# Perceiver block on one core: second-half attention scores placed directly ahead of the first value products, values computed in pairs, start-up loads cut smaller

## The reference

```python
x = x + xattn(layernorm(x), ctx)     # 32 query heads, 8 KV heads, head width 128, RoPE
x = x + attn(layernorm(x))           # 32 heads of width 16, biases
x = x + ffn(layernorm(x))            # base product + gated low-rank experts (8 of rank 16)
# xattn, for each KV head and its 4 query heads:
q, k, v = rope(xn @ Wq.T), rope(ctx @ Wk.T), ctx @ Wv.T
a = softmax(where(causal, q @ k.T * 128**-0.5, min))
out += (a @ v) @ Wd.T
```

## Time and profile before

| what | value |
|---|---|
| median of three runs | 716.91 us (lowest 716.67) |
| the profiled execution's own time | 717.73 us |
| its span, first to last instruction | 715.7 us |
| TensorE busy | 705.5 us, 99% |
| VectorE, GpSimd, ScalarE busy | 512.8, 472.1, 372.8 us |
| mean busy share of the 16 DMA engines on the loads' queue | 21.5% |

### The profile page before, as it was taken

How to read it: one execution, slowest core, us unless ns; L and a number is a source line. 1 busy time by engine, 2 the same in 40 slices (tenths; PEclk the granted TensorE clock), 3 DMA queues, 4 the chain that set the end, 5 groups by cost and what they waited for, 6 DMA issues and landing times.

```text
span 715.7 us, 12890 instructions
## 1 busy us (share of the span) xinstructions
PE 705.5 (99%) x4848; PEld 563.6 (79%) x4848; DVE 512.8 (72%) x814; ACT 372.8 (52%) x559; POOL 472.1 (66%) x360
## 2 busy tenths in 40 slices
PE   8999999899999999999999999999999999999998
PEld 6788878677778788787778778777788888887886
DVE  5665897957857857757767767758667888889735
ACT  5555665644644643743743743743336677765220
POOL 1898145777776877867867867844624889985730
PEclk9999999999999999999999999999999999999999
DMA  7554513411310310311301301300300110011003
GB/s 273 207 166 144 170 51 103 162 49 41 118 45 16 117 44 19 113 43 42 103 31 44 103 29 60 104 1 16 103 0 2 45 31 31 2 41 50 16 1 117
DMA packets 25560, 51.08 MB, mean 71 GB/s; under 512 B 2352, under 2 KB 10672, under 8 KB 25520
## 3 DMA queue, kind: packets, MB, share of 16 engines
q1 hardware_dynamic: 25520, 50.53, 21.5%
HBM read 40.04 MB, written 10.49 MB: 71 GB/s over the span
## 4 chain that ended last, share of the span: by engine, by line
PE 86%; DVE 6%; ACT 2%; DMA 2%; issue 2%; POOL 1%; SPq 0%; DVEq 0%; ACTq 0%
PE pj L1583 11%; PE sc L1674 11%; PE pj L1674 10%; PE pj L1773 9%; PE tp L1583 8%; PE pv L1661 5%; PE sc L1641 4%; PE tp L1674 4%; PE pj L1951 3%; PE pv L1569 3%; PE sc L1823 2%; PE tp L1836 2%; PE pv L1847 2%; PE tp L1557 2%; PE pj L1557 2%; PE tp L1648 2%
## 5 line engine op out<-in xcount | busy, mean ns | idle before, releaser
L494 POOL TENSOR_TENSOR sw<-sw,cst 128x512 f32<-128x512 f32 x72 | 102.4, 1422 | 39.5 <-ACT sw L671 39.4
L518 POOL TENSOR_TENSOR sm<-sm,mx 128x512 f32<-128x512 f32 x64 | 72.0, 1131 | 40.7 <-DVE mx L1209 27.3
L523 POOL TENSOR_TENSOR sm<-sm,rz 128x512 f32<-128x512 f32 x64 | 66.7, 1057 | 24.1 <-DVE rz L1224 24.1
L500 POOL TENSOR_TENSOR qr<-t,sw 128x512 f32<-128x512 f32 x54 | 73.5, 1362 | 7.7
L1583 PE MATMUL tp<-x,w 128*128 128x512 f32 x288 | 76.3, 401 | 1.2 <-ACT sw L671 0.8
L793 ACT ACTIVATE sm<-sm 128x512 f32<-128x512 f32 x64 | 40.3, 633 | 61.9 <-POOL sm L518 61.9
L512 POOL TENSOR_TENSOR w<-raw,w 128x896 fp32r<-128x896 f32 x24 | 50.4, 2120 | 33.1 <-ACT w L656 33.1
L1773 PE MATMUL pj<-xh,ws 128*128 128x512 f32 x192 | 64.6, 402 | 0.2 <-ACT kb L891 0.2
L1583 PEld LDWEIGHTS tp<-x,w 128*128 128x128 f32 x288 | 51.9, 188 | 11.8 <-ACT sw L671 1.0
L656 ACT ACTIVATE w<-raw 128x1792 fp32r<-128x1792 f32 x15 | 25.6, 1707 | 59.8 <-DVE raw L1099 59.8
L1228 DVE TENSOR_TENSOR cl<-pv,ch 128x1024 fp32r<-128x1024 f32 x32 | 39.1, 1222 | 23.2 <-ACT ch L801 23.2
(11 more groups left out here) (274 smaller groups left out, 1850.4 us busy)
## 6 DMA issues: line engine op xcount, KB each, us to landing
rawd<-in_w_d SPq DMA_DIRECT2D x16, 512.0 KB, 3.2
raw<-in_w_q SPq DMA_DIRECT2D x15, 512.0 KB, 3.3
kscr<-sm SPq DMA_DIRECT2D x16, 256.0 KB, 2.1
vscr<-sm SPq DMA_DIRECT2D x16, 256.0 KB, 2.6
kr<-kscr SPq DMA_DIRECT2D x8, 512.0 KB, 3.3
vv<-vscr SPq DMA_DIRECT2D x16, 256.0 KB, 2.6
raw<-in_w_k SPq DMA_DIRECT2D x4, 512.0 KB, 6.2
cT<-in_ctxT SPq DMA_DIRECT2D x4, 512.0 KB, 7.2
```

The costliest lines, as they stand in the source:

```text
L494: pool.tensor_tensor(bs(sw[par][:, :]), bs(sw[par][:, :]), rep(cst[:, C_SIN:C_SIN + S], HB), ALU.mult).then_inc(sin_done, 1)
L500: pool.tensor_tensor(o, bs(t1[par][:, :]), bs(sw[par][:, :]), ALU.add).then_inc(rope, 1)
L518: pool.tensor_tensor(s3, s3, per_group(mx[:, c, :], 8), ALU.subtract).then_inc(subbed, 1)
L523: pool.tensor_tensor(s3, s3, per_group(rz[:, c, :], 8), ALU.mult).then_inc(normed, 1)
```

## The change

- **Order in a head on TensorE.** Scores 2 and 3 move from behind the second product to behind S3, directly ahead of values 0. Values 0 and 1 follow each other, and so do values 2 and 3. Transposes 1 move ahead of S3, transposes 3 ahead of S3'.
- **Banks.** Values 1 are written into `tp` (B_BANK and T_BANK), values 3 into `sc`, and `c_hi` and `c_lo` read there. C_BANK and B_BANK trade places, and `out_x` gets other banks; waits are moved to match.
- **The other engines' orders** in `head` follow: the masks of chunks 2 and 3 stand behind c_mix and t1_q of k = 1, their exp between the high parts of values 0 and 1, their subtract_max between GpSimd's RoPE steps.
- **Start.** The first weight piece is loaded in halves and the first half of ctx in four slices of 256 KB; the constants are loaded earlier; the first K tiles multiply the parts in another order; seven fewer warm-up matmuls.
- **First head's queries and head 0.** first_swap(1) ahead of block_hi(6), the two c_add ahead of both first_t1, w7_sum(3) ahead of the last first_add, and another order of VectorE's work at the beginning of head 0.

```diff
@@ -34,7 +34,7 @@
 SCH = 4
 NSU = 2 * KT
 UNITS = [(0, 0), (1, 0), (0, 1), (1, 1), (2, 0), (3, 0), (2, 1), (3, 1)]
-WARM_UP = 16
+WARM_UP = 9
 C_ID, C_COS, C_SIN, C_MASK, C_PAR = 0, 128, 192, 256, 320
 NCONST = 322
 
@@ -119,7 +119,7 @@
...
@@ -268,9 +269,9 @@
 
 
         k_bank = [pj[:, 0, :], pj[:, 1, :], tp[:, 0, :], tp[:, 1, :]]
-        A_BANK, B_BANK, C_BANK, T_BANK = pj[:, 0, :], pj[:, 1, :], tp[:, 1, :], tp[:, 0, :]
-        O_BANK = [B_BANK, sc[:, 0, :], sc[:, 1, :], B_BANK, sc[:, 0, :], sc[:, 1, :], B_BANK, C_BANK]
-        O6_BANK = [B_BANK, sc[:, 0, :], sc[:, 1, :], B_BANK, sc[:, 0, :], A_BANK, B_BANK, C_BANK]
+        A_BANK, B_BANK, C_BANK, T_BANK = pj[:, 0, :], tp[:, 1, :], pj[:, 1, :], tp[:, 0, :]
+        O_BANK = [pv[:, 0, :], pv[:, 1, :], B_BANK, sc[:, 0, :], B_BANK, pv[:, 0, :], pv[:, 1, :], C_BANK]
+        O6_BANK = [pv[:, 0, :], pv[:, 1, :], B_BANK, sc[:, 0, :], B_BANK, A_BANK, B_BANK, C_BANK]
         O7_BANK = [B_BANK, A_BANK, C_BANK, B_BANK, A_BANK, C_BANK, B_BANK, C_BANK]
 
 
...
@@ -374,13 +375,14 @@
             def load_d(g, i):
                 sp.dma_start(rawd[i][:, :], w_d[g, i]).then_inc(s_rd[i], 16)
 
-            load_piece(0)
-            load_ctx(0, 0)
-            load_ctx(0, 1)
+            sp.dma_start(raw2[0][:, 0:512], w_k[0][:, 0:512]).then_inc(s_wa, 16)
+            for k in range(KT):
+                load_ctx(k, k, 1, 0)
+            sp.dma_start(raw2[0][:, 512:1024], w_k[0][:, 512:1024]).then_inc(s_w[0], 16)
             load_piece(1)
-            load_ctx(1, 0)
-            load_ctx(1, 1)
             sp.dma_start(cst[:, :], consts).then_inc(s_const, 16)
+            for i in range(2):
+                load_ctx(KT + i, 2 * i, 2, 1)
             sp.wait_ge(plo_d, 1)
             load_piece(2)
             sp.wait_ge(plo_p, 1)
...
@@ -557,13 +559,15 @@
                     subtract_max(4 * g + c, c)
                 for c in range(2):
                     normalise(4 * g + c, c)
-                for c in range(2, 4):
-                    subtract_max(4 * g + c, c)
                 for p in range(2):
                     for k in range(4):
                         rope_sin(k % 2, ri(2 * n + p, k))
+                        if p == 0 and k == 1:
+                            pool.wait_ge(scored, 4 * g + 4)
                         if more or p == 0 or k < 2:
                             rope_add(k % 2, ri(2 * n + p, k), q_out(p, k))
+                        if p == 0 and k < 2:
+                            subtract_max(4 * g + 2 + k, 2 + k)
                     if p == 0:
                         for c in range(2, 4):
                             normalise(4 * g + c, c)
...
@@ -708,12 +720,16 @@
                 act.wait_ge(stp, n)
                 act.activation(dst[:, :], bank, ACT.Copy).then_inc(pcp, 1)
 
-            piece_hi(0)
+            first_hi(0, s_wa, phi_a)
             ctx_hi(0, range(KT))
+            first_hi(1, s_w[0], phi)
             piece_hi(1)
             ctx_hi(1, range(KT))
+            swap_k(0)
             piece_hi(2)
-            for t, i in PHASE1:
+            swap_k(1)
+            piece_hi(3)
+            for t, i in PHASE1[2:]:
                 if t == "k":
                     if i == 4:
                         act.wait_ge(kproj, 6)
...
@@ -769,8 +783,8 @@
             block_hi(5)
             part_copy(pcb, 3, B_BANK)
             first_swap(0, C_BANK)
+            first_swap(1, T_BANK)
             block_hi(6)
-            first_swap(1, T_BANK)
             part_copy(u2, 5, A_BANK)
             part_copy(u2b, 6, B_BANK)
             part_copy(pc, 7, C_BANK)
...
@@ -819,27 +833,25 @@
                 if first:
                     turn(0, 0)
                     wdhi(g, 0, wdh)
-                    part_copy(u2, 14 * n + 3, A_BANK)
-                    p_copy(q, 0)
-                    part_copy(pc, 14 * n + 4, C_BANK)
-                    exp(q + 2, 2, X_SCALE)
-                    wdhi(g, 1, wdh)
                 else:
                     act.wait_ge(stp, 14 * n + 2)
                     wdhi(g, 0, wdh)
                     turn(0, 0)
-                    wdhi(g, 1, wdh)
+                    p_copy(q, 0)
                     part_copy(u2, 14 * n + 3, A_BANK)
-                    exp(q + 2, 2, X_SCALE)
+                if first:
+                    part_copy(u2, 14 * n + 3, A_BANK)
                     p_copy(q, 0)
-                    part_copy(pc, 14 * n + 4, C_BANK)
+                part_copy(pc, 14 * n + 4, C_BANK)
+                p_copy(q + 1, 1)
+                wdhi(g, 1, wdh)
+                turn(0, 1)
+                c_hi(q, 0)
+                exp(q + 2, 2, X_SCALE)
+                c_hi(q + 1, 1, tp4)
                 exp(q + 3, 3, X_SCALE)
-                c_hi(q, 0)
-                turn(0, 1)
-                p_copy(q + 1, 1)
                 turn(0, 2)
                 turn(0, 3)
-                c_hi(q + 1, 1)
                 part_copy(pc, 14 * n + 8, A_BANK)
                 if more:
                     w7_hi(2 * n + 2, 0, raw8, 14 * n + 7)
...
@@ -1182,6 +1206,7 @@
             block_lo(6)
             for p, (a, copy) in enumerate(((A_BANK, pc), (A2, pcb))):
                 c_add(9 + p, 5 + p, a, copy, cq[p])
+            for p in range(2):
                 dve.wait_ge(cadd, 3 + p)
                 first_t1(2 + p, cq[p][:, :])
             for p, a in enumerate((A_BANK, A2)):
@@ -1198,8 +1223,8 @@
             dve.wait_ge(cadd, 6)
             first_t1(7, C2, 4)
             first_add(6, 6)
+            w7_sum(3)
             first_add(7, 7)
-            w7_sum(3)
 
             def mask_max(n, c):
                 s3 = bs(sm4[c][:, :])
...
@@ -1262,33 +1287,37 @@
 
                 mask_max(q, 0)
                 mask_max(q + 1, 1)
-                sum_rec(q, 0)
-                c_mix(0, 0)
                 if first:
+                    c_mix(0, 0)
                     t1_q(0, 0)
+                    sum_rec(q, 0)
                     sum_rec(q + 1, 1)
-                    w7_lo(3, 1, 0)
-                    w7_lo(3, 1, 1)
                     for i in range(2):
                         dve.wait_ge(s_vs[i], 16 * NVT // 2)
                 else:
+                    sum_rec(q, 0)
+                    c_mix(0, 0)
                     sum_rec(q + 1, 1)
                     t1_q(0, 0)
+                wd_split(g, 0, wdh, wdl)
+                if first:
+                    w7_lo(3, 1, 0)
+                c_mix(0, 1)
+                t1_q(0, 1)
                 mask_max(q + 2, 2)
                 mask_max(q + 3, 3)
-                if not first:
-                    wd_split(g, 0, wdh, wdl)
-                c_mix(0, 1)
-                t1_q(0, 1)
+                c_lo(q, 0)
                 if first:
-                    wd_split(g, 0, wdh, wdl)
-                c_lo(q, 0)
-                wd_split(g, 1, wdh, wdl)
-                t1_q(0, 2)
+                    t1_q(0, 2)
+                    wd_split(g, 1, wdh, wdl)
+                    w7_lo(3, 1, 1)
+                else:
+                    wd_split(g, 1, wdh, wdl)
+                    t1_q(0, 2)
                 c_mix(0, 3)
                 t1_q(0, 3)
+                c_lo(q + 1, 1, tp4)
                 out_add(g, 0)
-                c_lo(q + 1, 1)
                 sum_rec(q + 2, 2)
                 sum_rec(q + 3, 3)
                 out_add(g, 1)
...
@@ -1530,31 +1559,44 @@
 
             def k_tile(ki):
                 g, h = K_TILES[ki]
...
@@ -1696,57 +1736,58 @@
                 pe.wait_ge(swp, ri(m, 0))
                 added(-1)
                 product(C_BANK, 0, W_12, X_21, True, True).then_inc(stp, 1)
-                if first:
-                    pe.wait_ge(rope, ri(m, 0))
-                scores_x(g, 2)
-                scores_x(g, 3)
                 pe.wait_ge(wlo, 2 * m + 2)
                 pe.wait_ge(pcp, 3 * m + 1)
                 product(A_BANK, 0, W_S2, X_T2, False, False).then_inc(stp, 1)
                 p_transposes(g, 0)
                 pe.wait_ge(swp, ri(m, 0) + 1)
                 product(C_BANK, 0, W_S1, X_T1, True, False).then_inc(stp, 1)
+                pe.wait_ge(tp_c, 4 * g + 1)
+                p_transposes(g, 1)
                 pe.wait_ge(pcp, 3 * m + 2)
                 product(A_BANK, 0, W_S3, X_T3, False, False).then_inc(stp, 1)
-                pv_x(g, 0)
+
+                if first:
+                    pe.wait_ge(rope, ri(m, 0))
+                scores_x(g, 2)
+                scores_x(g, 3)
+                added(-2)
+                pv_x(g, 0, pv)
+                pv_x(g, 1, tp)
                 pe.wait_ge(cadd, 3 * m + 2)
                 product(A_BANK, 0, W_22, X_T4, False, True).then_inc(stp, 1)
-                p_transposes(g, 1)
                 product(C_BANK, 0, W_S4, X_22, False, True).then_inc(stp, 1)
-                added(-2)
                 out_x(g, 0)
-                pv_x(g, 1)
                 m = 2 * n + 1
                 pe.wait_ge(wlo, 2 * m + 2)
                 free(m)
```

(28 more changed lines are left out.)

123 lines of the change are left out of this document (77 added, 46 removed).

## The result

The changed kernel takes 730.21 us (median of 4 runs, 728.23 to 732.65) against 717.06 us (4 runs) before: a ratio of 1.0187, 95% interval 1.0137 to 1.0237. One of the four runs before took 1846.62 us and is not in the ratio; the other three took 716.67 to 717.20. The change is slower, clear of the spread; whether by more than 2%, the interval leaves open. The profiled execution after took 728.41 us, its span is 726.3 us; that of before had 717.73 and 715.7.

The account below looks back on a forecast made before the run. TensorE, busy 99% of the span, was taken as the bound. Start -2.8, queries -1.2, head 0 +0.5 and heads 1 to 6 +15.0 gave +11.5 on 717.73, 729.2, less 0.8: 728 us, range 709 to 735.

Parts of the forecast that it names:

- (b): Heads 1 to 6, before product S1: without second-half scores as cover TensorE idles about 2 us; head period 1.4 us longer.
- (c): Heads 1 to 6, second pair's first product W_11: waits for turn(0,2) behind exp and subtract_max, 1.1 us per head.
- (a): Head loop on TensorE: ten fp32 groups become seven, gaining 0.66 us per head if nothing waits.
- Six heads: Heads 1 to 6 together: 6 x (1.4 + 1.1) = +15.0 us, ends +6 and +21.
- Start: First loads and K tiles: tile 0 ends at 8.0 to 9.0 instead of 11.56; -2.8 us, ends -3.6 and -0.9.
- Queries: Products of the other first head (95 to 121 us): two 0.46 waits go; -1.2 us, ends 0 and -1.7.
- Head 0: Head 0: S1 earlier, but a longer chain to W_11; +0.5 us, ends -2.0 and +1.5.
- The cover is not needed: Rival, heads: VectorE's chain speeds up and S1 is released at 6.9; 708 us, chance 0.17.
- Only the first wait: Rival, heads 1 to 6: W_11's chain overlaps more, heads cost 1.0 to 1.4 each; 720 or 721 us, chance 0.17.
- Mutual blocking: Rival, W_11's chain: rope_add meets wd_split, then wd_split meets subtract; 1.3 us more per head, 737 us, chance 0.13.

Follow-up runs that it names:

- e2: The changed kernel with ScalarE's turn(0,2) moved ahead of exp(q+3), TensorE's order as changed: 723.55 us (1.0095).
- e8: The changed kernel with wd_split(g,1) on VectorE right behind wd_split(g,0) in heads 1 to 6, wdhi(g,1) on ScalarE moved ahead too: 725.36 us (1.0123).
- e11: Against e4: wdhi(g,1) ahead of chunk 3's exp, c_hi of values 0 ahead of turn(0,1), wd_split(g,1) ahead of c_lo of values 0: 708.95 us (0.9879).
- e1: The changed kernel with TensorE's scores 2 and 3 back behind the second product, other engines as changed: 730.59 us (1.018).
- e3: The changed kernel with the edits of both e1 and e2: 713.68 us (0.9953).
- e4: The changed kernel with scores, masks, subtracts and exps of chunks 2 and 3 in the order of before on all engines: 713.74 us (0.9957).
- e6: The kernel before with the change's start alone (first loads, order of first K tiles, nine warm-ups): 714.48 us (0.9965).
- e5: The kernel before with the change's start and its order in the first head's queries, nothing in the heads: 714.13 us (0.9956).
- e9: The kernel before with the changes inside the heads alone, start and queries as before: 732.64 us (1.022).

## Why the prediction was right

- **(b) S1 without its cover: right.** Release at 8.87 us into the head, as (b) had it from the chain through four engines, and TensorE ready at 6.94, forecast 6.9 (transposes at 179.03, which occupy 0.40). From start to start that is 1.93 us idle, forecast 2; the row's 1.67 counts from a modelled end. Its price was put too high: 1.4 a head, ends 1.0 and 1.8, where e2, which has this wait alone, shows 0.93. The mis-sized term is what is left after S1, taken as 45.2: measured 46.04 less the second wait, 44.8, mostly because the four value steps take 0.96 to 0.97 each, not 1.07.
- **(c) The chain onto W_11': right in place and time.** Forecast 22.4 + 0.7 = 23.1, measured 23.07; the wait 1.1, measured 1.10 from a modelled end and 1.26 from start to start (the last output matmul starts at 194.07 and occupies 0.23). The doubling of rope_add was taken at +0.7 net and is 2.18 - 1.30 = 0.88 raw; e8 takes it away and 0.21 of the wait is left, near the 0.4 of (c) with nothing in the way. The rule of the Trainium skill in SBUF — State Buffer, "Who interferes with whom", holds in direction: the GpSimd add lengthens only where a VectorE instruction with two SBUF inputs runs beside it, and e8 moves the lengthening along with that instruction. Taken as the prediction took it, the loser losing the other's full 1.22, it gives more than the 0.88 measured. Taken as a wait for the end of the instruction that started first, it fits: wd_split still ran 1.04 when the add started (191.39 - 190.35). Which engine loses depends on which starts later; in e11 it was VectorE's split that lost 1.09 (last section).
- **What (b) and (c) did not say** is how they combine. They were summed as 1.4 + 1.1 = 2.5 per head; the period rose by 2.2 to 2.3. The two prices aren't independent: with the cover back and the second chain left, the head costs 2.24 (e1, 54.93 less 52.69), with the second chain gone and no cover 0.92 (e2, 53.61), with both undone 0.04 (e3, 52.73). The sum is allowed only in the order in which it was made, because (c) measured its wait from a TensorE already late by the first.
- **(a) Merged groups: the mechanism holds, and only half of it pays in this order.** Two value steps in one group are 0.97 apart (186.79 to 187.76) where 1.07 stood before, and a product that no longer stands behind an fp32 group takes 1.36 instead of 1.49 or more. But a pair pays only where TensorE does not wait after it. The second one (values 2 and 3) always did: from W_11' on a head is 0.5 shorter in the changed kernel, in e3 and in e4. The first one's gain was waited away and more, so that e3 and e4 gain nothing in the whole (52.73 and 52.82 against 52.69). In e11 the first half is as long as before the change (W_11' at 20.33 and 20.32), and all the gain, 0.6, next to (a)'s 0.66, stands in the second (31.75 instead of 32.37): values 2 and 3 take 1.93 instead of 2.13, S4' 1.36 instead of 1.57, out 4 to 7 10.97 instead of 11.15, W_11' 1.36 instead of 1.49, and S3' 0.10 more.
- **Six heads: +15.0 forecast, +15.5 measured**, of which 13.9 is waits and order and 1.6 the clock, which no term held. That the sum is this close is partly luck: a head of the loop cost 0.25 less than forecast, and head 6 and the clock made up for it.
- **Start: -2.8 forecast, -2.1 to -2.7 measured.** Tile 0's last part starts at 8.52 and is through at 9.44, not 8.0 to 9.0; before, it was at 11.56. The first query product starts 2.7 earlier (86.46 for 89.13). Alone the start is worth 2.6 us (e6). TensorE did not fall back to the warm-up's spacing: 1.09 for four matmuls is the usual 0.23 apart, with the modelled end of the last.
- **Queries: -1.2 forecast.** In the profile of the changed kernel the stretch from the first product (86.46) to the first scores is 30.01 us, before 31.79; but e6, without that order, has 30.76, e5, with it, 30.84, and their medians differ by 0.35. So the term is not shown to be more than nothing: the product near 99 lost its wait, as forecast, but without the move that was to do it. In the profile of the changed kernel the fourteen products run without any gap, 19.04 us from start to start (14 x 1.36); before they took 20.82.
- **Head 0: +0.5 forecast, -0.41 measured**, inside its ends. W_11' comes 24.15 us after the head's first scores (140.62 - 116.47), forecast 24.8. A wait that the prediction did not name stands in it, 2.59 us of transposes 0 on the first normalise: its sum_rec now comes behind c_mix and t1_q. With the second half's scores and softmax in the old order head 0 is shorter still (54.95 in e4, 117.23 to 172.18).
- **The rivals.** "The cover is not needed" failed for the reason given against it: sum and multiply come before chunk 2's mask, so nothing frees them. "Only the first wait" fell with the second one's 1.10. "Mutual blocking" did not occur in heads 1 to 6: rope_add lost once, the subtract behind it ran its usual 1.03. In head 0 it did, in the case that the rival named, rope_add (135.31) starting before wd_split (135.73): wd_split took 1.96, and the subtract that followed at 136.56 took 2.03 beside wd_split. The median is 2.2 us above the forecast, the profiled execution 0.8 below its 729.2. The changed kernel's four runs go with the clock: 728.23 and 728.41 at a mean granted clock of 0.998 and 0.997, 732.02 and 732.65 at 0.995 each. That spread the prediction did not have. On the profiled execution the terms measure -2.7 (start), -1.8 (queries' stage), -0.4 (head 0) and +15.5 (heads 1 to 6), 10.6 against 11.5 forecast. Some slips in its working change nothing (TensorE ready 13.18 behind S1's start, not 13.14, by its own terms; 739 for 740 at the high ends).

## What to carry to other kernels

Work that an engine does while a chain through other engines runs is cover: before moving it, find when the chain ends and what else the engine has until then. Two waits in one loop don't add up; undo them one at a time and together, since the later one may hide all that the first is worth (here 0.0, 1.3 and 2.2 us per head). And a saving on the engine that bounds the kernel is real only if the operands of its next steps come earlier too: the same paired values gave nothing in the whole of e4, and three moves on ScalarE and VectorE then took 4.8 us off (e11).

## What the runs showed of the hardware

**The granted clock fell after a wait inside a busy loop.** The table by stretches for head 2 of the changed kernel (TensorE's granted clock is the first number behind GpSimd's busy time, 1.00 being 2.4 GHz) and TensorE's timeline there:

```profile
227.40:236.00 8.60, 7.20 (x87) 5.59 (x86) 7.41 (x12) 3.66 (x6) 6.86 (x6) 1.00 0.16 61
236.20:240.20 4.00, 3.93 (x13) 3.21 (x14) 0.31 (x1) 2.47 (x6) 2.65 (x2) 0.61 0.00 0
...
244.00:283.00 39.00, 37.91 (x183) 30.45 (x182) 27.26 (x35) 18.70 (x25) 28.59 (x21) 1.00 0.19 67
```

```profile
236.27 2.27 PE L1625 MATMUL pj<-x,w 128*128 128x512 f32 x6 [1.68 <-ACT sw L683]
238.34 1.05 PE L1688 MATMUL tp<-cst,sm 128*128 128x128 f32 x4
```

In the middle of that stretch (238 to 240) the granted clock is 0.50, its lower level of 1.2 GHz; the product took 2.27 instead of 1.65 and the head 1.6 us more. It followed a wait of 1.68 us, which heads 1 to 5 of this kernel all have (head 6 waits 1.42), and came in one of them. A product as slow stands in the profiles of e2, in two heads, and of e9 (405.32, 2.09 us), each behind the same wait of 1.68:

```profile
289.99 2.34 PE L1625 MATMUL pj<-x,w 128*128 128x512 f32 x6 [1.68 <-ACT sw L683]
345.15 2.80 PE L1625 MATMUL pj<-x,w 128*128 128x512 f32 x6 [1.68 <-ACT sw L683]
```

In e1 the clock fell to 0.66 in the stretch behind the 2.15 us wait for W_11' of head 4. In e2, e8 and e9 it fell in head 0 too, behind waits of 2.60, 2.61 and 1.99 us for the first normalise; in e8 that is the only fall, and its five waits of 1.68 in the loop brought none. So of 30 waits of 1.6 us and more in the heads of these five profiles, eight were followed by a fall; in the profiles without such waits none was found, and two runs of e8 had a mean clock of 1.000 in spite of them. The mean granted clock of the profiled executions was 0.993 to 0.998 in the five kernels with such waits (the changed one, e1, e2, e8, e9) and 0.999 or 1.000 in the others. That the wait is the cause was not tried by itself, and what tells the eight from the rest is open.

**Whichever of VectorE and GpSimd starts later waits for most of what the other has left.** This is read from pairs of instructions with both inputs in SBUF. wd_split takes 1.22 us undisturbed, a subtract or normalise 1.05, a rope_sin or rope_add 1.30. In the changed kernel's rope_add (190.35) wd_split had 1.04 us to run and the add lost 0.88; in the subtract before the change (187.58), 1.06 and 0.90. Four more:

| the one that starts later | what the earlier one still runs | what it loses |
|---|---|---|
| wd_split, changed kernel, 179.91 | normalise, 0.61 | 0.47 |
| wd_split, e4, 189.49 | rope_add, 0.57 | 0.44 |
| wd_split, e11, 185.69 | rope_add, 1.22 | 1.09 |
| rope_add, e8, 185.83 | wd_split, 0.94 | 0.79 |

In all six the loss is 0.13 to 0.16 us less than what the earlier one still runs.
